# First query tiles' scores issued between the matmuls of two output tiles

## What is computed

```python
qkv = layernorm(x) @ w_qkv                     # 8 groups of 4 query heads, one key and one value head
scores = einsum('bqhgd,bkhd->bhgqk', q, k) * D ** -0.5
bias = where(rel >= 0, -slopes * sqrt(max(rel, 0)), -inf)
attn = softmax(scores + bias)                  # 256 x 256 a head, causal
x = x + einsum('bhgqk,bkhd->bqhgd', attn, v).reshape(B, S, NH * D) @ w_o
dots = softmax(layernorm(x) @ centroids.T / 0.1)   # 64 clusters
hits = dots > 0.01
out = where(hits.any(1)[:, None] & hits.any(0)[assignments][None, :], layernorm(x) @ weight.T + bias, 0)
x = x + out
```

## Time and profile before

| | us |
|---|---|
| median of 3 runs | 1258.83 |
| lowest and highest run | 1258.37, 1260.3 |
| span of the profiled execution | 1257.8 |
| PE busy | 1243.5 (99%) |
| PE weight loads busy | 1052.0 (84%) |
| DVE busy | 755.8 (60%) |
| ACT busy | 757.0 (60%) |
| POOL busy | 516.1 (41%) |

### The profile page before, as it was taken

How to read it: one execution, slowest core, us unless ns; L and a number is a source line. 1 busy time by engine, 2 the same in 40 slices (tenths; PEclk the granted TensorE clock), 3 DMA queues, 4 the chain that set the end, 5 groups by cost and what they waited for, 6 DMA issues and landing times.

```text
span 1257.8 us, 21956 instructions
## 1 busy us (share of the span) xinstructions
PE 1243.5 (99%) x6200; PEld 1052.0 (84%) x6200; DVE 755.8 (60%) x2150; ACT 757.0 (60%) x2171; POOL 516.1 (41%) x476
## 2 busy tenths in 40 slices
PE   9899999999999999999999999999999999999998
PEld 7788888888888888888888888888888888888787
DVE  7777555555655555556555555655555565676677
ACT  5877556666665566666555566665566666655543
POOL 4521726227432546226442465327362264224223
PEclk9999999999999999999999999999999999999999
DMA  6522334334342334333333343324243343422103
GB/s 201 168 94 92 122 104 150 117 108 150 93 132 98 116 127 145 114 114 123 114 117 100 129 142 120 126 90 130 96 149 117 108 150 112 138 68 90 62 17 134
DMA packets 162522, 147.15 MB, mean 117 GB/s; under 512 B 10048, under 2 KB 123968, under 8 KB 162496
## 3 DMA queue, kind: packets, MB, share of 16 engines
q1 hardware_dynamic: 156672, 128.48, 31.0%
q0 software_dynamic: 5824, 18.36, 4.9%
HBM read 84.67 MB, written 62.13 MB: 117 GB/s over the span
## 4 chain that ended last, share of the span: by engine, by line
PE 90%; DVE 4%; ACT 4%; issue 1%; DMA 0%; POOL 0%; DVEq 0%; SPq 0%; ACTq 0%
PE ps L1319 84%; PE ps L1420 3%; PE ps L1421 1%; ACT prob L731 1%; ACT prob L722 1%; PE ps L1339 1%; DVE ring_whole L985 1%; DVE stats L898 0%; PE ps L1349 0%; DVE qT_lo L960 0%; DVE prob L1022 0%; DMA acc<-in_L_attn_hidden_states 0%; DVE rs L927 0%; PE ps L1451 0%; ACT ring_whole L685 0%
## 5 line engine op out<-in xcount | busy, mean ns | idle before, releaser
L1319 PE MATMUL ps<-xnT,wqkv_hi 128*128 (+2 forms) x1560 | 480.3, 389 | 0.0
L551 POOL TENSOR_TENSOR ring<-ring_whole,pT_hi 128x512 fp32r<-128x512 f32 x189 | 244.0, 1291 | 476.2 <-ACT pT_hi L711 475.8
L1319 PEld LDWEIGHTS ps<-xnT,wqkv_hi 128*128 128x128 f32 x1560 | 289.7, 188 | 59.5 <-issue 1.6
L722 ACT ACTIVATE prob<-prob,negmax 128x128 f32<-128x128 f32 (+1 forms) x512 | 226.8, 444 | 180.8 <-DVE negmax L1022 180.0
L1319 PE MATMUL ps<-xnT,wqkv_lo 128*128 (+1 forms) x780 | 302.7, 388 | 0.0
L731 ACT ACTIVATE prob<-prob,rinv 128x128 f32<-128x128 f32 (+1 forms) x512 | 190.3, 445 | 62.4 <-DVE rinv L1030 62.4
L1319 PE MATMUL ps<-wo_hi,oT_hi 128*128 128x512 f32 x512 | 201.8, 394 | 0.0
L1319 PE MATMUL ps<-wo_lo,oT_hi 128*128 128x512 f32 x512 | 199.8, 390 | 0.0
L1319 PE MATMUL ps<-wo_hi,oT_lo 128*128 128x512 f32 x512 | 199.4, 389 | 0.0
L1319 PEld LDWEIGHTS ps<-xnT,wqkv_lo 128*128 128x128 f32 x780 | 146.4, 188 | 30.3
L1002 DVE TENSOR_TENSOR acc<-ps,acc 128x512 f32 (+1 forms) x128 | 88.5, 691 | 127.4 <-PE ps L1319 127.4
(11 more groups left out here) (148 smaller groups left out, 1730.7 us busy)
## 6 DMA issues: line engine op xcount, KB each, us to landing
turned<-ring_whole SPq DMA_DIRECT2D x189, 256.0 KB, 2.1
ring_whole<-turned SPq DMA_DIRECT2D x189, 256.0 KB, 3.0
turned_v<-vT SPq DMA_DIRECT2D x32, 256.0 KB, 2.0
vT<-turned_v SPq DMA_DIRECT2D x31, 256.0 KB, 2.7
raw<-in_L_attn_w_qkv POOLq DMA_DIRECT2D x28, 256.0 KB, 3.1
raw<-in_L_attn_w_o POOLq DMA_DIRECT2D x28, 256.0 KB, 3.3
raw<-in_L_attn_w_qkv POOLq DMA_DIRECT2D x28, 128.0 KB, 3.2
acc<-in_L_attn_hidden_states SPq DMA_DIRECT2D x3, 1024.0 KB, 7.7
```

Source lines behind the costliest of these rows:

```text
L551: pool.tensor_tensor(ring_slot(c), whole_slot(c), pT_hi[:, c % 2, :].bitcast(F32), ALU.subtract).then_inc(pT_lo_done, 1)
L722: ins = act.activation(s, s, ACT.Exp, bias=negmax[:, n:n + 1], scale=-1.0, accum_out=rowsum[:, n:n + 1])
L1319: ins = pe.matmul(dst, l, r, start=start and m == 0, stop=stop and m == n - 1)
```

## The change

A new helper `out_and_scores(u, k, i0)` issues output tile `k` and the two first-query-tile scores `i0` and `i0 + 1` in one interleaved order: for each of the four heads long, 256 columns, long, 128 columns, long. It replaces `project_out(u, 1)` with scores 0 and 1, and `project_out(u, 3)` with scores 4 and 5. Both of its waits for the score banks stand ahead of its first matmul. Scores 0 and 1 thereby move from ahead of `apply_v(u, 5)` into the second output tile, and 4 and 5 from ahead of the fourth output tile into it. In unit 0, which has no attention part, the scores are issued as before. In unit 30 the fourth output tile moves ahead of scores 6 and 7, and `dense(0, 2)` ahead of it. No other engine's code is changed.

```diff
--- before.py
+++ after.py
@@ -1424,6 +1424,28 @@
                                          True, True)
                 ins.then_inc(s_mm, 1)
 
+            def out_and_scores(u, k, i0):
+                pe.wait_ge(oT_lo_done, u * QTILES + k + 1)
+                for i in (i0, i0 + 1):
+                    pe.wait_ge(scores_biased, u * SCORE_BANKS + i - 1)
+                b = i0 // 4
+                q0 = b * SEQ
+                n = 0
+                for head in range(HPG):
+                    i, h = i0 + head // 2, head
+                    q_hi, q_lo = qT_hi[:, h, q0:q0 + P], qT_lo[:, h, q0:q0 + P]
+                    dst = ps[:, score_bank(u, i), (h % 2) * SEQ:(h % 2 + 1) * SEQ]
+                    o_hi, o_lo = oT_hi[:, k % 3, h * P:(h + 1) * P], oT_lo[:, k % 3, h * P:(h + 1) * P]
+                    bank = ps[:, out_bank(u, k), :]
+                    pe.matmul(bank, o_hi, wo_hi[:, h, :], start=h == 0, stop=False)
+                    pe.matmul(dst, q_hi, kT[:, 2 * b, :, :], start=True, stop=False)
+                    pe.matmul(bank, o_hi, wo_lo[:, h, :], start=False, stop=False)
+                    short = pe.matmul(dst[:, 0:P], q_lo, kT[:, 2 * b, 0, :], start=False, stop=True)
+                    if h % 2:
+                        short.then_inc(s_mm, 1)
+                    long = pe.matmul(bank, o_lo, wo_hi[:, h, :], start=False, stop=h == HPG - 1)
+                long.then_inc(wo_mm, 1)
+
             def cluster_logits(p, u):
 
                 pe.wait_ge(ln_lo_done, p * TPQ + TPQ * (QUADS + 1))
@@ -1516,8 +1538,9 @@
                     pe.wait_ge(qk_lo_done, u * 5 + 5)
                     if L is not None and attn:
                         pe.wait_ge(ln_lo_done, L * TPQ + TPQ)
-                    scores(u, 0)
-                    scores(u, 1)
+                    if not attn:
+                        scores(u, 0)
+                        scores(u, 1)
                 if attn:
                     apply_v(u, CHUNKS - 1)
                 if proj:
@@ -1525,9 +1548,7 @@
                 if p is not None:
                     cluster_logits(p, u)
                 if attn:
-                    if not proj:
-                        pe.wait_ge(added, u * QTILES)
-                    project_out(u, 1)
+                    out_and_scores(u, 1, 0)
                 if p is not None:
                     transpose_logits(p)
                 if p == 0:
@@ -1541,17 +1562,17 @@
                 if attn:
                     pe.wait_ge(added, u * QTILES + 1)
                     project_out(u, 2)
-                if proj:
+                if not attn:
                     scores(u, 4)
                     scores(u, 5)
                 if p == 0:
                     dense(p, 2)
+                if attn:
+                    pe.wait_ge(added, u * QTILES + 2)
+                    out_and_scores(u, 3, 4)
                 if p == 0:
                     scores(u, 6)
                     scores(u, 7)
-                if attn:
-                    pe.wait_ge(added, u * QTILES + 2)
-                    project_out(u, 3)
                 if p == 0:
                     dense(p, 3)
                 elif proj:
```

## The result

The changed kernel takes 1305.07 us (median of 4 runs, 1304.03 to 1306.6); the kernel before took 1259.2 us beside it (4 runs). The ratio is 1.0364 with a 95% interval of 1.035 to 1.0379: 45.9 us slower. The forecast was 1297.5 us, in a range of 1286 to 1310.

The account below looks back on a forecast made before the run. The prediction took TensorE's back-to-back issue (PE) to bound the kernel. Loop stalls 28.4, 0.4 more in units 1 and 2, units 30 and 31 9.3 and interleaving 0.6 made 38.7 us: median 1297.5 us, range 1286 to 1310.

Parts of the forecast that it names:

- nothing to win in the slots: Interleaved tiles: a 128-column matmul costs 0.115 us whatever stands behind it, since the next weights load only under it.
- loads-ahead rival: Interleaved tiles: weight loads run two matmuls ahead, each group gains 0.18 us, 11 us in all; 1289 us, chance 0.05.
- the stall: PE at scores 3 and 7, waiting for `add_bias` to free a bank: 0.49 us each, 28.4 us for 58.
- the logit chain: Units 30 and 31: logit transposes wait for a copy that now comes later, costing 4.2 us in each unit.
- the interleaving, 62 x 0.01 us: 62 interleaved groups: eight short matmuls take 0.94 us instead of 0.93, 0.6 us lost in all.
- My bound of 0.02 us for a group: The most that interleaving was to lose in one group; the other bound was a gain of 0.18 us.
- the clock, as a rival with a chance of 0.10: Units 30 and 31: each PE gap brings a slow stretch costing 2.3 us, perhaps twice that; 1302 to 1307 us.
- The rise of 0.3 us for the fourth tile's wait for `add_bias(3)`: Unit 31: the fourth tile now waits where only score 5 did, 0.3 us more, bounds 0 and 0.7.
- unit 30's stall at score 7: Unit 30, PE at score 7: one stall of 0.59 us, taken as 0.6 us in the sum.

Follow-up runs that it names:

- e1: The kernel before, with the 128-column matmuls of the first query tiles made 256 columns wide: 1261.71 us, ratio 1.0016 to the kernel before.
- e7: The changed kernel, with one short matmul behind each of the tile's first eight long ones, leaving four long ones last: 1271.34 us, ratio 1.0088 to the kernel before.
- e8: The changed kernel, with the short matmuls behind the third to tenth long one, leaving two long ones last: 1289.41 us, ratio 1.0232 to the kernel before.
- e9: The changed kernel, with the eight short matmuls in a row between the eleventh and twelfth long one: 1339.09 us, ratio 1.0626 to the kernel before.
- e4: The changed kernel, but in units 30 and 31 scores 0 and 1 and the second tile as before: 1293.15 us, ratio 1.0267 to the kernel before.
- e5: The changed kernel, with 17 unused matmuls ahead of the logit transposes of units 30 and 31: 1303.16 us, ratio 1.0352 to the kernel before.
- e6: The changed kernel, interleaving the first and third tiles instead, each score's bank wait at its own first matmul: 1313.38 us, ratio 1.0423 to the kernel before.
- e10: e6 with `add_out(2)` behind `add_bias(5)`, third-tile shorts behind its fourth long matmul, scores 0 and 1 as before in layernorm units: 1264.3 us, ratio 1.0036.
- e2: The changed kernel with only the second tile interleaved, scores 4 and 5 ahead of the fourth as before: 1286.11 us, ratio 1.0214 to the kernel before.

## Why the prediction came out as it did

**Right: nothing to win in the slots.** Each load starts with the matmul before its own, in the interleaved tile too, and e1 shows by itself that the columns of a 128-column matmul do not set its cost. The loads-ahead rival wanted a tile of 3.5 us; it took 3.71.

**Right: the stall.** 0.49 us forecast, 0.49 us read at score 7 above, 60 new waits, and every link of the chain (DVE's start, step, release) at its forecast length. e7, e8 and e9 moved it to 0, about 0.25 and up as the position of the last short matmul says.

**Right: the logit chain.** Each was to cost 4.2 us; the waits grew from 0.26 to 4.39 us, by 4.13. e4 took it away: with what follows from it, 11.9 us.

**Mis-sized: the interleaving, 62 x 0.01 us.** The tile was to take 3.66 us and takes 3.71, so 62 x 0.06 = 3.7 us were lost where the sum had 0.6. The 128-column slot is even a little shorter than I had it (load to load 0.11 us); it is the 512-column matmuls around it that start 0.23 to 0.24 us apart instead of 0.227. I took 0.227 us from a tile that stands behind other long matmuls; in the kernel before, the third tile, behind short ones, already has 0.232 us for its first five. So the term had a row that I didn't read. Why a long matmul is slower there is not settled, and e7's order loses only 0.03 us for a tile. My bound of 0.02 us for a group was too narrow: it knew no way in which a long matmul could get longer.

**Mis-sized: the clock, as a rival with a chance of 0.10.** It was no alternative to the gaps but comes with them, and the sum had it at nothing. The only row that I had was the start of the kernel, 36 transposes at which the clock reads full, and no gap as long as 4.4 us anywhere else. The rival named 2.3 us for each gap, 4.6 us or more in all; the traces show 2.8 us in unit 30 and 0.4 net in unit 31, 3.2 us. That its price is near the first of these is luck, since it was worked out from a stretch whose clock reads full. The measured 1305.07 us lies in the rival's band of 1302 to 1307, but the clock made only 3.2 us of the way there. My own expectation for e5, 5 us, took no account of the wait that PE then runs into.

**Unit 31.** The rise of 0.3 us for the fourth tile's wait for `add_bias(3)` is in the right place. The wait itself is 0.52 us, and 1.67 us at full clock, but part of it replaces waits that the old order had, 0.90 us ahead of score 4 and the stalls at scores 6 and 7. From the transposes to the end e5 is 0.45 us longer than before (1300.1 - 1220.94 = 79.16 against 78.71).

**The sum, once more.** 44.5 us of span: 58 stalls of 0.49 us are 28.4, the logit gaps 8.3, the interleaving some 3.7, the clock 3.2, unit 30's stall at score 7 and the rest of unit 31 some 0.9 (0.5 and 0.45); that is 44.5. The start of this execution was 0.6 us earlier than that of the kernel before (9.12 against 9.74 us), so behind it the changed kernel took 45.1 us more, of which these terms name 44.5. The stalls of units 1 and 2 have some 0.3 of the other 0.6 us: their four waits are recorded at 0.29 to 0.30 us, those of the loop at 0.22 to 0.23. Forecast without clock: 38.7; the interleaving (3.1 us more) and the clock (3.2) are what it lacked. The medians are 1.4 us further apart than the spans; the profiled run of the changed kernel was the fastest of its four.

## What to carry to other kernels

Before interleaving short matmuls with long ones, find what sets the slot of the short one: if its next weight load starts only with it, the order of its neighbours changes nothing, and widening it in one experiment shows that for little. What an interleaving does change is when the group's last matmul ends: count the microseconds from there to each consumer (the bank's next user, a chain through three engines) and from each consumer back to PE, which is worth more than the slots. When work moves on one engine, the other engines' written orders must move too, and a new idle gap of several microseconds on TensorE is to be priced with a stretch at the lower clock level at its end. Before a small difference is put down to the clock, the granted clock of every run is to be looked at, not only that of the profiled one.

## What the runs showed of the hardware

- Doubling the columns of a 128-column matmul with float32 operands, each with its own weight load, costs 0.008 us (e1).
- Behind short matmuls, 512-column ones start 0.23 to 0.24 us apart instead of 0.227 us: the first five of the third tile in the kernel before, and all of an interleaved tile. No run here isolates the cause.
- Gaps of 4.39 us on PE came with a granted clock of 0.50 for some 6.8 us in unit 30 and some 3.4 us in unit 31. In unit 30 it fell while PE was still idle, in unit 31 some 0.5 us after it had resumed; the stretch in unit 30 cost 2.8 us. With 17 filler matmuls in each gap the profiled execution kept 1.00 up to its last microsecond; two of the other three runs have a mean of 0.997.
- Shorter gaps came with it too in some executions: one of 2.34 us in unit 2 of e6 (0.50 from 106.5), and one of 2.67 us in e10. In e6 the same wait of 2.34 us in unit 30 left the clock full.
- The clock also fell with no gap: in the profiled e2, e4 and e10 some 3.4 us at 0.50 began at the end of a row of matmuls of 128 and 64 columns that PE ran back to back behind unit 31. The other nine profiled executions ran the same row at 1.00.
- The start of the kernel varies by 1 us between executions (first 12 transposes at 9.12 to 10.16 us), as much as some of the effects above.
